# Eight attention steps placed among the groups of rows by a table, five buffers for the last tanh, and the last sums made in place

## The chip, the core and the metric

The kernel runs on one core of one Trainium2 chip, as one launch. The metric is the device time of an execution in microseconds. Before the change it is 1671.74 us, the median of three runs (1670.36 to 1673.09). The core has five engines that run their own instruction streams and meet only at semaphores: TensorE (PE, matrix products, written to the eight banks of PSUM), VectorE (DVE), ScalarE (ACT), GpSimd (POOL) and SyncE (SP, which here only issues DMAs, in program order, each after the waits that stand before it).

## The reference

Two layers work on `x` of 8 batches x 512 tokens x 256. The change touches only the second layer's attention, its mixture of experts, and the final product of the two:

```python
def _L1_attn_ref(x, ln_scale, ln_bias, wq, wk, wv):          # 16 heads of 16
    xn = _layernorm(x, ln_scale, ln_bias)
    q, k, v = heads(xn @ wq), heads(xn @ wk), heads(xn @ wv)
    probs = jax.nn.softmax(einsum('bhid,bhjd->bhij', q, k) / sqrt(256), axis=-1)
    return einsum('bhij,bhjd->bhid', probs, v) + xn
def _L1_ffn_ref(x, Wr, rb, W1, W2, W3, Ws1, Ws2, Ws3):       # 8 experts, the best 2 of each token, 1 shared
    w_full = softmax weights of the best 2 experts, 0 for the others
    h = (x @ W1) * silu(x @ W3)                              # per expert, 256 -> 512
    out = sum over experts of w_full * (h @ W2)              # 512 -> 256
    return out + ((x @ Ws1) * silu(x @ Ws3)) @ Ws2
x = x + s * g        # x before the layer, s: attention, g: silu of the ffn's output
```

## The kernel before

The change lies in one function, `layer1_attend_and_feed`, the kernel's last stage (from 733 us to the end of the profiled execution). It interleaves two kinds of work on all engines, so that one fills the other's waits.

**Attention.** A *quarter* g (0 to 31) is four heads of one batch. It has 8 *steps* u (0 to 7). In a step PE multiplies queries and keys into a bank pair (`scores`, L1500), and ACT takes the exponential of 128 x 1024 (`exps`, L1643) into one of two `prob` tiles. After every two steps PE multiplies the probabilities with the values (`weigh`, L1510; it stands in the steps 1, 4, 5 and 7). The maxima of the rows are found ahead of time: one `maxima` per step, numbered i = 0 to 255, in which PE multiplies into the bank pair M (`a_max_bank`, L1479) and DVE reduces it (L1786). There is one M, so PE may start maxima i only when DVE has reduced i - 1. In the step u = 3 PE transposes the maxima of the next quarter (`transpose_max`, L1486), DVE splits them in two rows (`split_max`, L1793 and L1795), and SP writes them into the query tile (`max_rows`, L1275 and L1278). In the steps 1 and 2 the outputs are copied (`copy_o`, ACT L1648), transposed (`transpose_o`, PE L1517) and divided (`divide`, DVE L1800 and L1804), and POOL adds them into `x_rows` (`add_o`, L1394). Query and key tiles (`qa`, `ka`) have three buffers: `load_qk(g + 2)` (six DMAs L1259 and six L1263, 64 KB each) is issued at the first step of quarter g, once the scores of quarter g - 1 are done, and is first needed by the maxima with i = 8 (g + 2).

**Groups of rows.** A *group* e (0 to 27) is 512 rows that go through an expert: 8 with the shared expert, 20 with rows sorted by expert. All its products are made as three products of split numbers (L93). In each of the group's places k = 0, 2, 4, 6 PE makes a quarter of gate and value (`up_gate`, `up_value`: 24 products, written to `a_hidden_bank`), and in k = 1, 3, 5, 7 a quarter of the down product of group e - 1 (`down`, 12 products). In k = 7 PE first transposes the next group's rows into M (`transpose_x`, L1525), ACT and DVE split them (`high_x` L1665, `low_x` L1822), and no maxima is made (in k = 4 there are two). Weights are loaded to `a_raw` by SP (L1285), split by ACT (`high_w`, L1672) and by POOL (`low_w`, L1408) or DVE (`low_w2`, L1827). A new weight's load waits until the old one is split; that of the second w2 of a group waits for the `low_w2` that DVE makes in place 6, after `low_h` (L1817). Each engine's order is written out by hand; there is one quarter per group, with g = e and u = k. SP's order in a group is: `load_qk`, the next rows, w3 and w1 of the next group, `load_v`, w2, `max_rows`, w3, w1 and w2.

**The end.** The last group is e = 27, so quarters 28 to 31, which is 32 steps, run after it. The down products of group 27 are made in quarter 28. Then ACT weights them (L1691), POOL adds them to the output array `fs` in memory by an indirect DMA (L1416), SP waits for these DMAs (`f_out`) and loads `fs` back in 8 batches (L1338; three semaphores, so batch 3 waits until batch 0 has landed), and for each batch b ACT takes tanh (`half_tanh`, L1679) and DVE does three operations (`last`, L1831, L1834 and L1839): (tanh + 1) x fs, times 0.5 x `x_rows`, plus `x1`. The tanh has two buffers, so that of batch b waits for the sum of batch b - 2. The sums go to three buffers, and SP stores each (L1347). DVE makes `last(0)` to `last(4)` after place 6 of quarter 30, `last(5)` and `last(6)` after that of quarter 31, and `last(7)` after `divide(31)`. From quarter 28 on the scores use two bank pairs, since the gate's banks are free.

## Time and profile before

| | us |
|---|---|
| median of three runs | 1671.74 |
| the profiled execution | 1671.11 |
| its span, first to last instruction | 1669.4 |
| PE busy in the span | 1505.7 (90%) |
| DVE, ACT, POOL busy | 1160.4, 963.8, 814.9 |
| mean granted TensorE clock | 0.956 of full |

A busy share is an average over stages. What is to be read here are two stretches: from 1090 to 1577 us, where groups of rows and attention run together, and from 1577.4 us (the first scores of quarter 28) to the end at 1669.4 us, where attention and the last sums run.

### The profile page before, as it was taken

The page shows a single profiled execution, that of the slowest core. Times are in us where ns is not written, and L with a number is a line of the kernel's source. Part 1 is how long each engine was busy: PE and PEld are TensorE (multiplying, and loading weights), DVE is VectorE, ACT ScalarE, POOL GpSimd, SP SyncE. Part 2 cuts the span into 40 slices and gives each one's busy share as a digit, 9 for nine tenths or more (in the row PEclk, how much of TensorE's full clock was granted, in tenths as well). Part 3 has the DMA queues.
Part 4 walks back from the last instruction along what each step waited for, and adds up shares of the span by engine and source line. Part 5 has one row for each costly group of instructions (what it writes and reads, how often), then busy time and mean ns, then how long its engine had stood idle before and what let it go on. Part 6 is the DMA issues. An engine that isn't in the chain of part 4 may idle for free.

```text
span 1669.4 us, 27215 instructions
## 1 busy us (share of the span) xinstructions
PE 1505.7 (90%) x9542; PEld 1128.7 (68%) x9542; DVE 1160.4 (70%) x1802; ACT 963.8 (58%) x1526; POOL 814.9 (49%) x755
## 2 busy tenths in 40 slices
PE   6589999999998379779999999999999999999976
PEld 3267877877787368647777777777777777777631
DVE  6667657757766388578776667777777777777657
ACT  3464565566454255434454567767677676777644
POOL 6424564554543278510255534656556655565410
PEclk9899999999999689969999999999999999999985
DMA  6716556553433579641455546766657677576563
GB/s 229 235 56 159 132 107 173 114 149 92 114 102 51 136 259 325 242 114 51 125 148 153 162 135 170 188 164 167 179 157 194 154 176 188 150 191 155 120 208 138
DMA packets 185384, 261.20 MB, mean 156 GB/s; under 512 B 36128, under 2 KB 117024, under 8 KB 185248
## 3 DMA queue, kind: packets, MB, share of 16 engines
q1 hardware_dynamic: 157216, 219.53, 43.8%
q0 software_dynamic: 28032, 39.93, 13.0%
q8 instruction: 77, 1.26, 0.3%
q14 instruction: 59, 0.48, 0.1%
HBM read 174.30 MB, written 84.56 MB: 155 GB/s over the span
## 4 chain that ended last, share of the span: by engine, by line
PE 39%; DVE 6%; SPq 3%; DMA 3%; issue 2%; ACT 2%; another core or an unknown queue 0%; POOL 0%; DVEq 0%; ACTq 0%; POOLq 0%
PE a_hidden_bank L93 16%; PE a_bank L93 8%; PE a_bank L1510 5%; PE a_max_bank L1479 5%; PE a_score_bank L1500 3%; DVE a_neg_max L1786 2%; DMA a_ka<-qk 2%; SPq L1259 1%; PE a_max_bank L1525 1%; SPq L1263 1%; PE a_bank L1517 1%; DVE a_w21lo L1827 1%; DVE a_hT1lo L1817 1%; ACT a_xThi L1665 1%; DVE a_w20lo L1827 1%
## 5 line engine op out<-in xcount | busy, mean ns | idle before, releaser
L1643 ACT ACTIVATE a_prob<-a_score_bank 128x1024 f32<-128x1024 f32 x240 | 246.2, 1026 | 244.7 <-PE a_score_bank L1500 198.6
L1786 DVE TENSOR_REDUCE a_neg_max<-a_max_bank 128x2 f32<-128x1024 f32 x249 | 304.1, 1221 | 82.4 <-PE a_max_bank L1479 70.5
L1416 POOL DMA_INDIRECT fs<-a_y,a_token x80 | 128.7, 1609 | 182.5 <-ACT a_y L1691 159.2
L619 POOL DMA_INDIRECT f<-e_ye,c_slot_row x64 | 104.6, 1635 | 128.7 <-ACT e_ye L530 65.6
L1479 PE MATMUL a_max_bank<-a_ka,a_qa 48*128 48x512 f32 x498 | 127.1, 507 | 27.8 <-DVE a_neg_max L1786 17.1
L1510 PE MATMUL a_bank<-a_prob,a_va 128*32 128x512 f32 x1024 | 143.3, 633 | 0.8 <-ACT a_prob L1643 0.6
L1809 DVE SCALAR_TENSOR_TENSOR a_tg<-a_tg,a_hidden_bank 128x512 f32<-128x512 f32 x112 | 76.7, 685 | 75.6 <-ACT a_tg L1653 71.0
L708 DVE TENSOR_TENSOR e_h<-e_bank,e_sge 128x512 f32<-128x512 f32 x64 | 44.3, 692 | 113.0 <-ACT e_sge L517 112.1
L1500 PE MATMUL a_score_bank<-a_qa,a_ka 50*128 50x512 f32 x480 | 100.5, 415 | 4.7 <-ACT a_prob L1643 2.4
L1479 PEld LDWEIGHTS a_max_bank<-a_ka,a_qa 48*128 48x128 f32 x498 | 47.5, 187 | 74.0 <-DVE a_neg_max L1786 31.1
L364 PE MATMUL e_bank<-m_wqkv,x_rows 128*128 128x512 f32 (+1 forms) x256 | 89.4, 492 | 4.6 <-ACT e_qkv L467 2.9
L1653 ACT ACTIVATE a_tg<-a_hidden_bank 128x512 f32<-128x512 f32 x112 | 67.2, 600 | 44.4 <-PE a_hidden_bank L93 38.2
L517 ACT ACTIVATE e_sge<-e_bank 128x512 f32<-128x512 f32 x64 | 38.2, 597 | 93.1 <-PE e_bank L93 92.0
L93 PE MATMUL a_hidden_bank<-a_xThi,a_w31hi 128*128 128x256 f32 x288 | 90.1, 313 | 0.0
L93 PE MATMUL e_bank<-e_w3hi,e_heThi 128*128 128x256 f32 x256 | 77.5, 303 | 13.6 <-DVE e_heTlo L712 13.6
L1813 DVE TENSOR_TENSOR a_h<-a_hidden_bank,a_tg 128x512 f32<-128x512 f32 x112 | 77.5, 692 | 15.3 <-PE a_hidden_bank L93 4.1
L93 PE MATMUL a_hidden_bank<-a_xThi,a_w11hi 128*128 128x256 f32 x288 | 85.0, 295 | 0.0
L611 POOL DMA_INDIRECT e_xg<-xn,c_slot_row x64 | 73.0, 1140 | 20.5 <-issue 19.2
L93 PE MATMUL a_hidden_bank<-a_xThi,a_w31lo 128*128 128x256 f32 x288 | 82.9, 288 | 0.0
L93 PE MATMUL a_hidden_bank<-a_xTlo,a_w31hi 128*128 128x256 f32 x288 | 82.7, 287 | 0.0
L93 PE MATMUL a_hidden_bank<-a_xTlo,a_w11hi 128*128 128x256 f32 x288 | 82.0, 285 | 0.0
L93 PE MATMUL a_hidden_bank<-a_xThi,a_w11lo 128*128 128x256 f32 x288 | 81.7, 284 | 0.0
(370 smaller groups left out, 4909.1 us busy)
## 6 DMA issues: line engine op xcount, KB each, us to landing
a_raw<-in_W SPq DMA_DIRECT2D x120, 512.0 KB
e_raw<-in_w SPq DMA_DIRECT2D x48, 512.0 KB, 4.1
a_qa<-qk SPq DMA_DIRECT2D x192, 64.0 KB
a_ka<-qk SPq DMA_DIRECT2D x192, 64.0 KB
xs<-c_pad SPq DMA_DIRECT2D x20, 516.0 KB
a_xg<-xs SPq DMA_DIRECT2D x20, 516.0 KB
qk<-p_hi SPq DMA_DIRECT2D x32, 256.0 KB, 4.0
qk<-p_lo SPq DMA_DIRECT2D x32, 256.0 KB, 4.3
```

What stands on the lines that cost most here:

```text
L93: ins = nc.tensor.matmul(out, a[i][x], b[l][y], start=first and n == m == 0, stop=last and n == len(pairs) - 1 and m == 2)
L364: ins = nc.tensor.matmul(bank[:, 0:f1 - f0], m.xnT[:, n, ch, t * P:(t + 1) * P], m.wqkv[:, ch, f0:f1], start=ch == 0, stop=ch == DC - 1)
L611: nc.gpsimd.indirect_dma_start(xg[u][:, t, :], None, xn_rows, bass.IndirectOffsetOnAxis(k.slot_row[:, e, t:t + 1], 0)).then_inc(xg_in[u], 16)
L619: nc.gpsimd.indirect_dma_start(f_rows, bass.IndirectOffsetOnAxis(k.slot_row[:, e, t:t + 1], 0), ye[:, t, :], None, compute_op=ALU.add).the ...
L1416: nc.gpsimd.indirect_dma_start(f_rows, bass.IndirectOffsetOnAxis(token[x % 4][:, t:t + 1], 0), y[:, t, :], None, compute_op=ALU.add).then_ ...
L1479: nc.tensor.matmul(max_bank(g, m)[:, s, :], qa[q][rows, p, t * P:(t + 1) * P], ka[q][rows, p, :], start=True, stop=True).then_inc(p1_ps, 1)
L1500: nc.tensor.matmul(score_bank(g, u)[:, s, :], ka[q][rows, p, j * P:(j + 1) * P], qa[q][rows, p, :], start=True, stop=True).then_inc(s_ps, 1)
L1510: ins = nc.tensor.matmul(OB[rows, :], va[g % NR][:, j, rows], prob[j % 2][:, h_, :], start=j == 0, stop=j == T - 1, tile_position=(0, 32 * ...
L1643: nc.scalar.activation(prob[j % 2][:, 2 * p:2 * p + 2, :], score_bank(g, u)[:], ACT.Exp, scale=float(D) ** -0.5).then_inc(p_done, 1)
L1786: nc.vector.tensor_reduce(neg_max[:, g % 2, :, T * p + t], max_bank(g, m)[:], AX.X, ALU.max, negate=True).then_inc(mx_done, 1)
L1809: nc.vector.scalar_tensor_tensor(tg[:], tg[:], 1.0, GATE[:], ALU.add, ALU.mult).then_inc(act_done, 1)
L1813: nc.vector.tensor_tensor(h[:], VALUE[:], tg[:], ALU.mult).then_inc(h_done, 1)
```

## The change

**A table of steps.** `steps` lists, for each of the 256 attention steps n = 8 g + u, the group and place (e, k) beside which it runs. The odd groups from 13 to 27 get a ninth entry with k = None: a step of attention with no group work, after place 7. So attention runs ahead of the groups by one step more after each, and 24 instead of 32 steps are left after group 27 (`freed` = 232). Up to group 13 the step u of a place k is the same as before; after that u = k + 1 (groups 14 and 15), k + 2 (16 and 17), and so on to k + 7 (26 and 27). `made[n]` is how many maxima have been made ahead of step n: 13 + n, and one more in the places 5, 6 and 7 and for the second maxima of place 4. Every engine's loop now runs over the table; work of the attention is tied to u, work of the groups to k. On SP `load_qk`, `load_v` and `max_rows` come at u = 0, 1 and 3, ahead of the group's loads of the same step.

**The end.** All eight loads of `fs` are issued at once, with one semaphore each for batch 0 and batch 1, one for 2 and 3, one for the rest. The tanh has five buffers (the three `raw` tiles, `xg` and `y`), and the product and the sum are written to `k.rows[:, b]`, from which they are stored. The tanh of batch 0 to 3 stands after the steps 247 to 250, that of 4 to 7 after 252 to 255; `last(0)` to `last(4)` stand in DVE's order at the steps 247, 249, 251, 253 and 255, the others behind them, with `divide(31)` ahead of `last(7)`.

```diff
-    th, sums = [raw[i][:].rearrange("p a f -> p (a f)") for i in range(2)], [raw[2][:].rearrange("p a (h d) -> p (a h) d", d=D), xg[:, :, 0:D], y[:]]
-    AHEAD = 3
+    th = [*(raw[i][:].rearrange("p a f -> p (a f)").rearrange("p (t d) -> p t d", d=D) for i in range(3)), xg[:, :, 0:D], y[:]]
+    TH = len(th)
...
+    rests = range(NF - 15, NF, 2)
+    steps = []
+    for e in range(G):
+        steps += [(e, k_) for k_ in range(NU)] + [(e, None)] * (e in rests)
+    steps = steps[:NU * G]
+    made = [LEAD]
+    for e, k_ in steps:
+        made.append(min(made[-1] + {4: 2, 7: 0}.get(k_, 1), NU * G))
+    freed = steps.index((NF, 0))
+    turned = [0] + [made[steps.index((e - 1, NU - 1))] for e in range(1, NF)]
...
@@ SP @@
-            for g in range(G):
-                e = g
-                if g + 2 < G:
+            for n, (e, k_) in enumerate(steps):
+                g, u = divmod(n, NU)
+                if u == 0 and g + 2 < G:
                     load_qk(g + 2)
-                store(e - 2, 1)
-                if group(e + 1):
-                    load_x(e + 1)
-                if NB <= e + 1 < NF:
+                if u == 1 and g + 2 < G:
+                    load_v(g + 2)
+                if u == 3 and g + 1 < G:
+                    max_rows(g + 1)
+                if k_ == 0:
+                    store(e - 2, 1)
+                    if group(e + 1):
+                        load_x(e + 1)
...
+                if k_ == 2 and NB <= e + 1 < NF:
                     load_w(0, weights(e + 1, 0))
                     load_w(1, weights(e + 1, 0))
...
+                if k_ == 3 and NB <= e < NF:
                     load_w(2, weights(e, 0))
...
                     for b in range(NB):
-                        sp.wait_ge(fs_in[b % AHEAD], 16 * (b // AHEAD))
-                        sp.dma_start(tiles(fs[b]), at(fs_b, b)).then_inc(fs_in[b % AHEAD], 16)
+                        sp.dma_start(tiles(fs[b]), at(fs_b, b)).then_inc(fs_in[batch_set(b)], 16)
...
@@ PE @@
+            for n, (e, k_) in enumerate(steps):
+                g, u = divmod(n, NU)
...
+                if k_ == 7 and group(e + 1):
                     transpose_x(e + 1)
+                if made[n + 1] > made[n]:
+                    maxima(made[n])
+                scores(g, u)
+                if u == 1 and g:
+                    weigh(g - 1, 3)
+                if u == 2 and g:
+                    transpose_o(g - 1)
+                if u == 3:
+                    transpose_max(g + 1)
+                if u in (4, 5):
+                    weigh(g, u - 4)
+                if u == 7:
+                    weigh(g, 2)
+                if k_ in (0, 2, 6) and group(e):
+                    up_gate(e, k_ // 2)
+                    up_value(e, k_ // 2)
...
+                if k_ in (1, 3, 5, 7) and group(e - 1):
+                    down(e - 1, k_ // 2)
...
@@ ACT @@
-                if b >= 2:
-                    act.wait_ge(sum_done, b - 1)
-                nc.scalar.activation(th[b % 2], fs[b], ACT.Tanh, scale=0.5).then_inc(th_done, 1)
+                if b >= TH:
+                    act.wait_ge(fin_done, 2 * (b - TH) + 2)
+                nc.scalar.activation(th[b % TH], tiles(fs[b]), ACT.Tanh, scale=0.5).then_inc(th_done, 1)
...
@@ DVE @@
-                nc.vector.scalar_tensor_tensor(th[b % 2], th[b % 2], 0.5, flat(k.rows[:, b]), ALU.mult, ALU.mult).then_inc(fin_done, 1)
+                nc.vector.scalar_tensor_tensor(k.rows[:, b], th[b % TH], 0.5, k.rows[:, b], ALU.mult, ALU.mult).then_inc(fin_done, 1)
                 dve.wait_ge(fin_done, 2 * b + 2)
                 dve.wait_ge(x1_in, 16 * NB)
-                if b >= 3:
-                    dve.wait_ge(out_done[b % 3], 16 * (b // 3))
-                nc.vector.tensor_tensor(sums[b % 3], tiles(th[b % 2]), tiles(x1[b]), ALU.add).then_inc(sum_done, 1)
+                nc.vector.tensor_tensor(k.rows[:, b], k.rows[:, b], tiles(x1[b]), ALU.add).then_inc(sum_done, 1)
```

Three places show what the table moves. On PE, between the last down product of place 7 of group 17 and the first gate product of group 18 (`a_max_bank` is a maxima, `a_score_bank` scores), there stood before:

```order
L93 MATMUL a_bank<-a_w21hi,a_hT0lo 128x256
L1479 MATMUL a_max_bank<-a_ka,a_qa 128x512 x2
L1500 MATMUL a_score_bank<-a_qa,a_ka 128x512 x2
L93 MATMUL a_hidden_bank<-a_xThi,a_w30hi 128x256
L93 MATMUL a_hidden_bank<-a_xTlo,a_w30hi 128x256
```

and now stand

```order
L93 MATMUL a_bank<-a_w21hi,a_hT0lo 128x256
L1497 MATMUL a_max_bank<-a_ka,a_qa 128x512 x2
L1519 MATMUL a_score_bank<-a_qa,a_ka 128x512 x2
L1536 MATMUL a_bank<-c_ident,a_oT 128x128 x4
L1497 MATMUL a_max_bank<-a_ka,a_qa 128x512 x2
L1519 MATMUL a_score_bank<-a_qa,a_ka 128x512 x2
L1504 MATMUL a_bank<-c_ident,a_neg_max 16x128
L93 MATMUL a_hidden_bank<-a_xThi,a_w30hi 128x256
L93 MATMUL a_hidden_bank<-a_xTlo,a_w30hi 128x256
```

Two maxima now stand close behind each other, with scores and a transpose between them and no product of a group. On DVE, at the same place (`a_xTlo` are the next rows, `a_w20lo` the w2 that place 6 splits), before:

```order
L1822 TENSOR_TENSOR a_xTlo<-a_max_bank,a_xThi 128x512 x2
L1817 TENSOR_TENSOR a_hT1lo<-a_h,a_hT1hi 128x2x256
L1827 TENSOR_TENSOR a_w20lo<-a_raw,a_w20hi 128x1024
L1786 TENSOR_REDUCE a_neg_max<-a_max_bank 128x2
L1809 SCALAR_TENSOR_TENSOR a_tg<-a_tg,a_hidden_bank 128x512
```

and now

```order
L1791 TENSOR_TENSOR a_xTlo<-a_max_bank,a_xThi 128x512 x2
L1786 TENSOR_TENSOR a_hT1lo<-a_h,a_hT1hi 128x2x256
L1796 TENSOR_TENSOR a_w20lo<-a_raw,a_w20hi 128x1024
L1755 TENSOR_REDUCE a_neg_max<-a_max_bank 128x2 x2
L1769 RECIPROCAL a_den<-a_bank 128x16
L1773 TENSOR_TENSOR a_o<-a_bank,a_den 128x256
L1778 SCALAR_TENSOR_TENSOR a_tg<-a_tg,a_hidden_bank 128x512
```

The first of the two reductions still stands behind the split of w2, and the second follows it at once. On SP, in group 22 (`a_raw` are weights, the one of 128x4x256 is w2; `a_vr` values, `a_mh` and `a_ml` the rows of maxima), before:

```order
L1285 DMA a_raw<-in_W 128x2x512
L1270 DMA a_vr<-v 128x4x64
L1283 TENSOR_LOAD c_owner
L1283 ISA x2
L1285 ISA
L1285 DMA a_raw<-in_W 128x4x256
L1275 DMA a_qa<-a_mh 1x8x128 x2
```

and now

```order
L1300 DMA a_raw<-in_W 128x2x512
L1274 DMA a_qa<-qk 16x2x512 x6
L1278 DMA a_ka<-qk 16x2x512 x6
L1298 TENSOR_LOAD c_owner
L1298 ISA x2
L1300 ISA
L1300 DMA a_raw<-in_W 128x4x256
L1285 DMA a_vr<-v 128x4x64
L1290 DMA a_qa<-a_mh 1x8x128 x2
```

The queries and keys of a quarter, which stood at the group's beginning, now come behind w3 and w1 and ahead of w2; in other groups they stand elsewhere in SP's order, by where u = 0 falls.

## Rows read from the trace of the kernel before

**Rows 1.** Windows: busy us of each engine (instructions), granted clock, DMA share, GB/s.

```profile
1577.40:1669.40 92.00, 60.75 (x309) 22.98 (x305) 58.72 (x61) 45.39 (x52) 15.64 (x13) 0.74 0.55 172
```

**Rows 2.** Timeline of PE, group 26 to 27: start, us, line, tiles [idle before].

```profile
1545.20 0.50 PE L1500 MATMUL a_score_bank<-a_qa,a_ka 50*128 50x512 f32 x2
1545.63 1.06 PE L1510 MATMUL a_bank<-a_prob,a_va 128*32 128x512 f32 x8
1548.26 0.50 PE L1479 MATMUL a_max_bank<-a_ka,a_qa 48*128 48x512 f32 x2
1548.60 0.39 PE L1500 MATMUL a_score_bank<-a_qa,a_ka 50*128 50x512 f32 x2
```

**Rows 3.** Timeline of DVE at the same place.

```profile
1547.86 0.69 DVE L1817 TENSOR_TENSOR a_hT0lo<-a_h,a_hT0hi 128x512 fp32r<-128x512 f32 x1 [0.63 <-ACT a_hT0hi L1659]
1548.47 1.22 DVE L1827 TENSOR_TENSOR a_w20lo<-a_raw,a_w20hi 128x1024 fp32r<-128x1024 f32 x1
1549.60 1.22 DVE L1786 TENSOR_REDUCE a_neg_max<-a_max_bank 128x2 f32<-128x1024 f32 x1
```

**Rows 4.** Timeline of PE: the two transposes of a quarter, in group 27.

```profile
1555.92 0.66 PE L1517 MATMUL a_bank<-c_ident,a_oT 128*128 128x128 f32 x4
...
1560.03 0.28 PE L1486 MATMUL a_bank<-c_ident,a_neg_max 128*16 128x128 f32 x1
```

**Rows 5.** Timeline of SP: starts of issues in groups 26 and 14.

```profile
1520.60 2.83 SPq L1259 DMA_DIRECT2D a_qa<-qk  x6
...
1528.58 2.73 SPq L1285 DMA_DIRECT2D a_raw<-in_W  x2
...
1534.09 0.39 SPq L1285 DMA_DIRECT2D a_raw<-in_W  x1
...
1158.22 4.94 SPq L1259 DMA_DIRECT2D a_qa<-qk  x6
```

**Rows 6.** Timeline of PE: maxima of places 2, 3, 5 and 6 of group 26.

```profile
1525.57 0.50 PE L1479 MATMUL a_max_bank<-a_ka,a_qa 48*128 48x512 f32 x2
...
1529.69 0.50 PE L1479 MATMUL a_max_bank<-a_ka,a_qa 48*128 48x512 f32 x2
...
1537.31 0.50 PE L1479 MATMUL a_max_bank<-a_ka,a_qa 48*128 48x512 f32 x2
...
1540.59 0.50 PE L1479 MATMUL a_max_bank<-a_ka,a_qa 48*128 48x512 f32 x2
```

**Rows 7.** Timeline of PE: two maxima that waited for keys.

```profile
1168.68 0.51 PE L1479 MATMUL a_max_bank<-a_ka,a_qa 48*128 48x512 f32 x2 [1.29 <-DMA a_ka<-qk]
...
1587.39 0.73 PE L1479 MATMUL a_max_bank<-a_ka,a_qa 48*128 48x512 f32 x2 [3.61 <-DMA a_ka<-qk]
```

**Rows 8.** Waits from 1100 to 1577 us: who for whom, us, times, longest.

```profile
PE a_max_bank L1479 <- DMA a_ka<-qk: 3.9, 6, 1.3
```

**Rows 9.** Windows: the stretch around the wait at 1587 us.

```profile
1585.00:1592.00 7.00, 4.61 (x25) 3.46 (x29) 3.07 (x5) 1.96 (x4) 0.68 (x1) 0.76 0.31 72
```

**Rows 10.** Timeline of SP and ACT, the last stretch.

```profile
1578.62 2.82 SPq L1259 DMA_DIRECT2D a_qa<-qk  x6
...
1615.37 0.33 SPq L1338 DMA_DIRECT2D a_w11hi<-fs  x1
...
1622.61 1.06 ACT L1679 ACTIVATE a_raw<-a_w11hi 128x1024 f32<-128x1024 f32 x1 [4.68 <-DMA a_w11hi<-fs]
...
1625.12 0.32 SPq L1338 DMA_DIRECT2D a_xTlo<-fs  x1
```

**Rows 11.** Timeline of PE and DVE, the last stretch.

```profile
1594.87 0.50 PE L1479 MATMUL a_max_bank<-a_ka,a_qa 48*128 48x512 f32 x2 [1.35 <-DVE a_neg_max L1786]
...
1629.92 1.20 DVE L1831 SCALAR_TENSOR_TENSOR a_raw<-a_raw,a_w11hi 128x1024 f32<-128x1024 f32 x1
...
1633.56 1.22 DVE L1831 SCALAR_TENSOR_TENSOR a_raw<-a_raw,a_w11lo 128x1024 f32<-128x1024 f32 x1
...
1660.69 0.26 DVE L1800 RECIPROCAL a_den<-a_bank 128x16 f32<-128x16 f32 x1 [3.88 <-PE a_bank L1517]
```

More of the change, by code:

```diff
@@ new lines, in _ @@
+            final = {freed + i: b for b, i in enumerate((15, 16, 17, 18, 20, 21, 22, 23))}
+            for n, (e, k_) in enumerate(steps):
+                g, u = divmod(n, NU)
+                fresh, coming = NB <= e < NF, NB <= e + 1 < NF
+                if k_ == 7 and group(e + 1):
+                    high_x(e + 1)
+                exps(g, u)
+                if u == 1 and g:
+                    copy_o(g - 1)
+                if k_ == 0:
+                    if group(e - 2):
+                        weighted(e - 2, 1)
+                    if group(e):
+                        tanh(e, 0)
+                    if fresh:
+                        high_w(0, weights(e, 1))
+                if k_ == 1:
+                    if group(e):
+                        high_h(e, 0)
+                    if fresh:
+                        high_w(1, weights(e, 1))
+                if k_ == 2:
+                    if e == 0:
+                        high_w(2, 0)
+                    if NB <= e - 1 < NF:
+                        high_w(2, weights(e - 1, 1))
+                    if group(e):
+                        tanh(e, 1)
+                if k_ == 3:
+                    if group(e):
+                        high_h(e, 1)
+                    if group(e - 1):
+                        weighted(e - 1, 0)
+                if k_ == 4:
+                    if group(e):
+                        tanh(e, 2)
+                    if coming:
+                        high_w(0, weights(e + 1, 0))
+                if k_ == 5:
+                    if group(e):
+                        high_h(e, 2)
+                    if coming:
+                        high_w(1, weights(e + 1, 0))
+                if n == NU + 5:
@@ L1770, in _ @@
-                exps(g, 7)
-                if group(e):
+                if k_ == 6:
+                    if group(e):
+                        tanh(e, 3)
+                    if fresh:
+                        high_w(2, weights(e, 0))
+                if k_ == 7 and group(e):
                     high_h(e, 3)
-                if e == NF + 1:
-                    half_tanh(0)
+                if n in final:
+                    half_tanh(final[n])
             copy_o(G - 1)
@@ L1930, in _ @@
             for m in range(NU):
-                maxima(0, m)
+                maxima(m)
             split_max(0)
-            for m in range(5):
-                maxima(1, m)
-            for g in range(G):
-                e = g
-                maxima(g + 1, 5)
-                if group(e):
+            for m in range(NU, LEAD):
+                maxima(m)
+            ending = {freed + i: b for b, i in enumerate((15, 17, 19, 21, 23))}
+            for n, (e, k_) in enumerate(steps):
+                g, u = divmod(n, NU)
+                if made[n + 1] > made[n]:
+                    maxima(made[n])
+                if u == 2 and g:
+                    divide(g - 1)
+                if u == 3:
+                    split_max(g + 1)
+                if k_ == 0 and group(e):
@@ L1951, in _ @@
-                if g:
-                    divide(g - 1)
-                if e == 0:
+                if n == 2:
                     low_w2(0)
-                if g == 1:
+                if n == NU + 2:
                     route_logit(1)
-                if g == 2:
+                if n == 2 * NU + 2:
                     route_slot(0)
-                if group(e):
+                if k_ == 2 and group(e):
                     hidden(e, 1)
-                maxima(g + 2, 0)
-                split_max(g + 1)
```

317 lines of the change are left out of this document (106 added, 211 removed).

## The prediction

> **What bounds the kernel now.** I read the page's busy lines first, then the clock and the windows by stage, then, at the seams that the table touches, the timelines of PE, DVE and SP, and last the waits. In the stage of groups and attention PE has no slack: a group takes some 30 us and PE's waits in 477 us of it are a few for keys and a few tenths elsewhere; those for keys sum to 3.9 us [rows 8]. So what PE must do or wait for there is time. After group 27 it is different: in 92.0 us PE is busy for 60.8 and the granted clock is 0.74 [rows 1]. There a chain sets the pace: down products of group 27, the add to `fs`, its loads, the tanh, eight times `last` on DVE. The change takes eight steps from the second stage to the first. The question is what a step costs beside PE's full list, and whether the last stage is paid by the step at all.
>
> **What an added step costs: work.** A step is one maxima and one scores, 0.34 us from start to start and about as much again [rows 2], so 0.7. Eight times that is 5.6. The added steps have u = 0 to 7, once each, so four of them weigh (1.06, some 1.0 of which is PE's own pace [rows 2]), one has the 0.6 transpose and one the 0.3 [rows 4]: 4.9. Together 10.5 us, at the full clock.
>
> **The wait between two maxima.** Take the scores of place 7 as time zero (1545.20). In the next step PE makes its maxima at 3.06, one weigh included [rows 2], but DVE reduces it only from 1549.60 to 1550.82, since `low_h` and the split of w2 stand ahead of it [rows 3]: until 5.6. Today 3 us of gate and value products cover that. In the added step nothing does: the next maxima needs the one M, and in the order there is only a scores between them. Another maxima that stood like this waited 1.35 us [rows 11]. So the second maxima starts at 5.7. PE is through at 2.0 (3.06 less the weigh) plus 0.7, plus what place 7 and the added step have of weighs and transposes: a gap of 3.0 less that. By u of the added step: 0: 2.0; 1: 2.0; 2: 1.4 and 0.5 more because the copy of the outputs (ACT) stands ahead of `high_h`; 3: 2.1 and 0.7 more for a `divide` behind the split; 4: 1.7 and 0.5 for `split_max`; 5: 1.0 and 0.4 (the exponential waits for a weigh); 6: 2.0. Sum 14.3. The eighth, after group 27, has no next rows and takes the place of a wait that is there today: 0.2 more than its work. Bounds: 8 if DVE's chain moves forward wherever ACT has less to do, 18 if it slips by another half microsecond each.
>
> **Two more seams.** With the shift, u = 2 falls on place 7 of group 18, so `divide` runs behind the split of w2 and ends at about 5.2, while PE stands at `transpose_max`, which needs it, at 3.3: 1.9. With u = 3 on place 7 of group 20 `split_max` ends at 5.05, and the weigh of the next step stands ready at 3.0: 2.0. Together 3.9; bounds 0 (if POOL's and ACT's lists give way) and 6.
>
> **The keys.** This is the largest term that the order alone doesn't show. Today `load_qk` starts when SP gets past the load of the second w2: 1520.60 in group 26 [rows 5], and is needed in place 3, at 1529.69 [rows 6], 9.1 us later. When PE did wait, the keys had taken 10.5 us (1158.22 to 1168.68) and 8.8 (1578.62 to 1587.39) [rows 5, 7]. I take 9.1: today they come just in time. The shift moves the need, not always the issue.
> - u = 0 on place 7 (groups 14, 15): SP is still behind the same w2, so the issue stays, but the need is a place earlier, 1525.57 instead of 1529.69 [rows 6]: 4.1 each. In the step after group 13 itself the seam's wait leaves 0.9.
> - u = 0 on place 4 (20, 21): SP is held by the first w2 until 1534.09 [rows 5] and issues behind it at 1534.5. Through the places 5 to 7 maxima run one ahead, so the need is place 6, 1540.59 [rows 6]: 6.1 us, short by 3.0 each.
> - u = 0 on place 3 (22, 23): behind w3 and w1, issued from 1528.58 to 1531.3 [rows 5], need in place 5, 1537.31 [rows 6]: 6.0, short by 3.1 each.
> - On places 6, 5, 2, 1 the issue is held only by the scores of the step before and has over 10 us: nothing.
>
> Sum 0.9 + 8.2 + 6.0 + 6.2 = 21.3, less the 3.9 that PE waits for keys today [rows 8], which falls away or is part of it: 17.4. Bounds: 5 (keys in 7 us, where no weight is ahead of them) and 28 (10.5 us). The weights that such a load pushes back (w2 in groups 22 and 23, by 3.4 us) are wanted by ACT only in place 6, and come just in time.
>
> **The clock.** After the wait of 3.61 us the two maxima took 0.73 instead of 0.50 [rows 7], and the granted clock of the 7 us around it is 0.76 [rows 9], so part of it ran at 1.2 instead of 2.4 GHz. Up to the next full-speed work that lost about 1.2 us. Seven new waits are of 1 to 4 us; I count 1.2 for half of the five or so longest: 3.0 (bounds 0 and 8). The Trainium skill (TensorE: Matmul & The Clock Gate, "What's actually happening") says that the gate follows how busy the array has been and halves the clock when it was idle. By it alone a wait costs more than its own length, and the trace agrees for the one of 3.61; for the short ones of [rows 8] it shows no loss.
>
> Rows in all: 10.5 + 14.3 + 0.2 + 3.9 + 17.4 + 3.0 = 49.3 us more until the scores after group 27.
>
> **What the last stage gets back.** Its first 8 steps are as before. The load of the last keys now starts about 1 us before the stage's zero and not 1.2 after (1578.62 against 1577.4 [rows 10]), because a step stands between it and the w2 that held it: the wait of 3.61 shrinks by 2.1, and 0.3 goes at the next maxima. The chain over POOL's add is unchanged. The `x1` loads no longer stand behind a `load_qk`, so they are out of the way when `fs` is loaded. Today batch 0 takes from 1615.37 to 1622.61, while two later batches were 2.5 us apart for two (1622.61 to 1625.12), 1.26 each [rows 10]. Alone it should land in some 3.5: 3.7 less. So the tanh of batch 0 comes at 45.2 (1622.61 less 1577.4) - 2.4 - 3.7 = 39.1 after the stage's zero and `last(0)` 1.1 later, at 40.2. Today DVE starts it at 52.5 (1629.92 [rows 11]), for it stands behind `divide(29)`; that wait of about 6 us goes. From there DVE bounds: a `last` takes 3.64 (1629.92 to 1633.56 [rows 11]), seven are 25.6, `divide(30)` 0.7, and from `divide(31)` to the end of the span it takes 8.7 as today (1660.69 to 1669.4): 35.0 instead of 39.5, the wait of 3.88 [rows 11] being gone. The remaining steps, 8 exponentials and 7 tanh of about 1 us and four weighs at the low clock, need under 20 and hide behind these 25.6. The five buffers are what lets ACT run ahead; that the sums are written elsewhere costs DVE nothing. The stage: 40.2 + 35.0 = 75.2 instead of 92.0, 16.8 less (bounds 11 and 21).
>
> The Trainium skill (DMA: Bandwidth & Descriptors, "Queues, rings and completion order") says that an engine takes the descriptors of one ring in order. By it batch 0 lands first though eight are issued at once; if they shared instead, it would land after 8 x 1.26 = 10.1 us and the gain be 6.6 smaller. The trace has three batches in flight, and shows them landing one after another, so I keep the smaller number.
>
> **The sum.** +49.3 - 16.8 = +32.5 us. The profiled execution took 1671.1 us (span 1669.4 and 1.7 around it), 0.6 less than the median. That gives 1703.6; I say 1703.
>
> **The rivals.**
> - *The keys come in time.* For it: in six waits of the whole stage the longest is 1.3 us, so the transfer may often be well under 9.1, and without weights ahead it has the 16 engines for itself. Against: the six that did wait show 8.8 to 10.5. Then 17.4 and the clock's 3.0 fall away: +28.9 - 16.8 = +12, 1683.
> - *Faster.* The mechanism: in the seam the reduction starts early enough, or PE had hidden slack there, so that a step costs its 10.5 / 8 = 1.3 us, and keys are in time; and the last stage is paid by the step, 92.0 / 32 = 2.9 each, 23 in all: -12.5, 1659. It decides from the point where the waits between two maxima and for keys together stay under 6 us. For it: ACT, DVE and the low clock do make a step dear there. Against: the chain over `fs` and the eight `last` does not have those steps in it.
> - *Dearer still.* The keys take 10.5 us as in group 14 (7 x 1.3 = 9 more) and the clock falls after each long wait (5 more): 1717.
>
> **Chances.** Forecast 0.60, keys in time 0.17, dearer 0.16, faster 0.07. What a measurement can tell from no change is 0.2%, 3.3 us. Faster than that 0.07, within it 0.03 (the low end of the second case), slower 0.90. The forecast's own range is 1693 to 1712. The one for 8 in 10 takes in most of the cheap case and the dear one's start: 1682 to 1716.
>
> **What would show it.** PE waiting for `a_neg_max` at eight places after groups 13, 15, ..., 27, by 1 to 3 us; PE waiting for `a_ka` in the groups after 14 and 15 by about 4 and in 20 to 23 by about 3; the stage's zero at 1627 instead of 1577; from there 75 us to the end, `last(0)` at 40, DVE then without a gap over 1 us but one. It is wrong if the waits for keys sum to under 8 us, if the two maxima stand under 2.2 us apart, or if the last stage gives back more than 25.

## The result and the profile after

The changed kernel takes 1727.4 us, the median of four executions (1719.0 to 1729.4), the kernel before, measured beside it, 1671.1 us (four). The ratio is 1.033, 95% interval 1.029 to 1.037. Forecast were 1703 us and a range of 1682 to 1716: the direction is right, the size is not. Of all executions in this document one, the fourth of e5_keys_where_shifted, took 1918 us at a granted clock of 0.736, and it is left out of every comparison.

The profiled execution is the shortest of the four, 1719.0 us with a span of 1717.3; the span grew by 47.9 us against a forecast of 32.5. Three windows say where. The first row is of before, from the transposes of group 14's rows (place 7 of group 13) to the last stage's zero, and the others are of after: the same stretch, and from that zero, the first scores after group 27's last work and the step behind it, to the end. Columns: window, its length, busy us of PE, its weight loads, DVE, ACT and POOL (instructions), granted clock, DMA share, GB/s.

```profile
1152.18:1577.40 425.22, 419.88 (x3120) 311.27 (x3120) 315.54 (x396) 298.81 (x407) 240.37 (x165) 1.00 0.65 167
```

```profile
1149.68:1641.98 492.30, 448.53 (x3190) 328.20 (x3189) 323.09 (x408) 305.25 (x416) 237.96 (x167) 0.96 0.58 146
...
1641.98:1717.30 75.32, 42.62 (x240) 16.67 (x236) 47.09 (x48) 36.60 (x43) 14.50 (x11) 0.75 0.61 198
```

The last stage answers to [rows 1]: 75.3 us instead of 92.0, as forecast (75.2). The stretch of rows is 67.1 us longer; it began 2.5 us earlier in this execution, so the zero moved by 64.6, where 49.3 had been forecast. The row splits the 67.1 in two. PE stood idle for 43.8 us (492.30 less 448.53) instead of 5.3, which is 38.4 more. And it was busy for 28.7 us more, though the added work was put at 10.5. The granted clock fell from 1.00 to 0.96, and the other 18.2 us are the same work at the half clock: in the clock's own record PE works for 37.8 us of the stretch at 1.2 GHz, which loses half of that, 18.9.

The idle time, by what PE waited for in that stretch (columns: who for whom, us in all, times, longest); it answers to [rows 8], where keys took 3.9 us in six:

```profile
PE a_max_bank L1497 <- DMA a_ka<-qk: 20.5, 6, 4.7
PE a_max_bank L1497 <- DVE a_neg_max L1755: 11.1, 8, 1.9
PE a_bank L1529 <- DVE a_ml L1764: 4.7, 2, 2.3
PE a_bank L1504 <- DVE a_o L1773: 4.2, 2, 2.1
PE a_max_bank L1497 <- issue: 1.8, 1, 1.8
PE a_score_bank L1519 <- ACT a_prob L1636: 1.3, 2, 0.8
```

One by one, in the timeline of PE (start, us, line, tiles, idle time before and what ended it); they answer to [rows 7]:

```profile
1156.32 0.51 PE L1497 MATMUL a_max_bank<-a_ka,a_qa 48*128 48x512 f32 x2 [1.89 <-DVE a_neg_max L1755]
1200.64 0.80 PE L1497 MATMUL a_max_bank<-a_ka,a_qa 48*128 48x512 f32 x2 [4.70 <-DMA a_ka<-qk]
1228.51 0.50 PE L1497 MATMUL a_max_bank<-a_ka,a_qa 48*128 48x512 f32 x2 [1.76 <-DVE a_neg_max L1755]
1235.87 0.50 PE L1497 MATMUL a_max_bank<-a_ka,a_qa 48*128 48x512 f32 x2 [1.66 <-DMA a_ka<-qk]
1326.93 0.27 PE L1504 MATMUL a_bank<-c_ident,a_neg_max 128*16 128x128 f32 x1 [2.08 <-DVE a_o L1773]
1360.38 0.27 PE L1504 MATMUL a_bank<-c_ident,a_neg_max 128*16 128x128 f32 x1 [2.07 <-DVE a_o L1773]
1389.31 0.75 PE L1497 MATMUL a_max_bank<-a_ka,a_qa 48*128 48x512 f32 x2 [3.64 <-DMA a_ka<-qk]
1426.33 0.50 PE L1497 MATMUL a_max_bank<-a_ka,a_qa 48*128 48x512 f32 x2 [3.25 <-DMA a_ka<-qk]
1463.94 0.50 PE L1497 MATMUL a_max_bank<-a_ka,a_qa 48*128 48x512 f32 x2 [2.94 <-DMA a_ka<-qk]
1499.53 0.80 PE L1497 MATMUL a_max_bank<-a_ka,a_qa 48*128 48x512 f32 x2 [4.33 <-DMA a_ka<-qk]
```

The six waits for keys are in groups 15, 16, 20, 21, 22 and 23, where the forecast had put all but one small one. The wait at 1228.51, of 1.76 us, shows what the forecast missed. The last of these windows is behind it, the first three are behind the long one at 1200.64:

```profile
1201.00:1203.00 2.00, 2.00 (x10) 1.35 (x9) 1.41 (x2) 1.07 (x2) 0.05 (x1) 0.50 0.69 228
1203.00:1205.00 2.00, 2.00 (x12) 2.00 (x11) 0.28 (x1) 1.12 (x2) 1.34 (x4) 0.50 0.01 2
1205.00:1207.00 2.00, 2.00 (x19) 1.49 (x18) 1.27 (x2) 0.37 (x1) 0.00 (x0) 0.98 0.03 6
...
1230.00:1232.00 2.00, 2.00 (x11) 2.00 (x11) 0.99 (x3) 1.20 (x3) 0.00 (x0) 0.50 1.08 263
```

PE is busy for all of each 2 us but gets through 10 to 12 matmuls at 0.50, which is 1.2 GHz, and 19 at full clock. There are ten such stretches in the rows' part: five at waits for keys (2.94 to 4.70 us), five behind waits in the seams (1.76 to 2.33 us). They cost some 1.8 us each (18.2 / 10).

The last stage, in the timelines of ACT, DVE and SP, answers to [rows 10, 11]:

```profile
1677.30 0.33 SPq L1355 DMA_DIRECT2D a_w11hi<-fs  x1
...
1681.48 1.06 ACT L1672 ACTIVATE a_raw<-a_w11hi 128x1024 f32<-128x1024 f32 x1 [5.48 <-DMA a_w11hi<-fs]
...
1682.57 1.23 DVE L1800 SCALAR_TENSOR_TENSOR a_raw<-a_raw,a_w11hi 128x1024 f32<-128x1024 f32 x1 [11.78 <-ACT a_raw L1672]
...
1711.71 1.23 DVE L1803 SCALAR_TENSOR_TENSOR x_rows<-a_raw,x_rows 128x1024 f32<-128x1024 f32 x1 [0.68 <-POOL x_rows L1409]
```

The load of batch 0 lands 4.2 us after its issue instead of 7.2, `last(0)` starts at 40.6 after the zero and 34.7 us remain. Behind it DVE has one gap, of 0.68 us.

### The profile page after: what moved, and what is told of

The parts are those of the page before. It is cut to its first block, busy times and chain, and to the rows that moved or that the text cites. A ratio compares the mean times of both kernels' runs of the same rounds, so it can differ in the third digit from the quotient of the medians.

```text
span 1717.3 us, 27212 instructions
## 1 busy us (share of the span) xinstructions
PE 1517.0 (88%) x9542; PEld 1140.8 (66%) x9542; DVE 1157.3 (67%) x1802; ACT 961.3 (56%) x1526; POOL 809.5 (47%) x755
## 4 chain that ended last, share of the span: by engine, by line
PE 39%; DVE 6%; DMA 3%; SPq 3%; issue 3%; ACT 2%; POOL 0%; ACTq 0%; DVEq 0%; POOLq 0%
PE a_hidden_bank L93 17%; PE a_bank L93 7%; PE a_bank L1529 5%; PE a_max_bank L1497 5%; PE a_score_bank L1519 3%; DMA a_ka<-qk 2%; PE a_max_bank L1545 1%; SPq L1274 1%; DVE a_neg_max L1755 1%; SPq L1278 1%; DVE a_w20lo L1796 1%; PE a_bank L1536 1%; ACT a_prob L1636 1%; DVE x_rows L1803 1%; ACT a_xThi L1658 1%
## 5 line engine op out<-in xcount | busy, mean ns | idle before, releaser
L1636 ACT ACTIVATE a_prob<-a_score_bank 128x1024 f32<-128x1024 f32 x244 | 250.1, 1025 | 266.6 <-PE a_score_bank L1519 210.7
L1782 DVE TENSOR_TENSOR a_h<-a_hidden_bank,a_tg 128x512 f32<-128x512 f32 x112 | 77.5, 692 | 14.3 <-PE a_hidden_bank L93 2.8
L1409 POOL TENSOR_TENSOR x_rows<-x_rows,a_o 128x256 f32<-128x256 f32 x32 | 29.8, 932 | 119.9 <-DVE a_o L1773 119.8
L611 POOL DMA_INDIRECT e_xg<-xn,c_slot_row x64 | 73.1, 1142 | 20.4 <-issue 19.2
```

The costliest lines, as they stand in the source:

```text
L611: nc.gpsimd.indirect_dma_start(xg[u][:, t, :], None, xn_rows, bass.IndirectOffsetOnAxis(k.slot_row[:, e, t:t + 1], 0)).then_inc(xg_in[u], 16)
L1636: nc.scalar.activation(prob[j % 2][:, 2 * p:2 * p + 2, :], score_bank(NU * g + u)[:], ACT.Exp, scale=float(D) ** -0.5).then_inc(p_done, 1)
L1782: nc.vector.tensor_tensor(h[:], VALUE[:], tg[:], ALU.mult).then_inc(h_done, 1)
```

## The experiments

Three questions were open: whether the six waits for keys and the seams cost what they seem to, what eight steps really return at the end, and whether a wait alone makes the clock fall. Theory at the start: rows and end are separate sums, and each wait costs its length and something for the clock. The main rival: the added steps cost so much for a reason that no single wait shows. Ratios are to the kernel before in the same batch of runs, with 95% intervals. Diffs are against the changed kernel unless another is named.

**e1_end_only: no added steps, the new end.**

```diff
-    rests = range(NF - 15, NF, 2)
+    rests = ()
...
-            final = {freed + i: b for b, i in enumerate((15, 16, 17, 18, 20, 21, 22, 23))}
+            final = {freed + i: b for b, i in enumerate((15, 16, 17, 18, 20, 24, 26, 28))}
...
-            ending = {freed + i: b for b, i in enumerate((15, 17, 19, 21, 23))}
+            ending = {freed + i: b for b, i in enumerate((19, 21, 23, 25, 27))}
```

> The changed kernel with an empty list of rests, so no added step: the groups run as before and 32 steps are left behind group 27. Kept: eight loads of fs at once, five tanh buffers, sums in the rows' tile. The tanh of the batches stand after the steps 15 to 18, 20, 24, 26 and 28 of the last stage and last(0) to last(4) at its steps 19, 21, 23, 25 and 27. Theory (the last stage is set by the chain of fs, tanh and eight last, not by its steps): last(0) starts at 48 to 50 us of the stage instead of 52.5 and runs without the wait of 3.9, so about 8 us faster than before, 1663 (1658 to 1667). Rival (what the last stage gave back was eight steps fewer): no gain, 1671 within 3. Second rival: the chip's time of the last stage falls by the full 15 us without the table, 1656.

Measured: 1670.2 us against 1673.8, ratio 0.997 (0.995 to 0.999). A gain between the rival's none and the theory's 8 us. Its last stage and the first `last`:

```profile
1588.65:1675.60 86.95, 55.31 (x309) 21.59 (x305) 58.53 (x61) 44.84 (x52) 15.65 (x13) 0.81 0.56 182
```

```profile
1640.97 1.20 DVE L1800 SCALAR_TENSOR_TENSOR a_raw<-a_raw,a_w11hi 128x1024 f32<-128x1024 f32 x1
```

The stage is 5.1 us shorter than before (92.0). The tanh of batch 0 (1634.12) comes 7.0 us after the issue of its load (1627.08); that this is due to the `x1` loads ahead of it is an inference here, which e8 tests. And `last(0)` starts at 52.3, still behind `divide(29)` and `split_max`. What the eight added steps return beside this end is then the difference to after: 86.95 less 75.32, 11.6 us, 1.45 a step. Their work is 10.5. So even at no wait at all they would have been worth 1 us, and less beside a better end (e8).

**e2_keys_first: all key loads ahead of the weights.** On SP, in every group:

```diff
-                if k_ == 2 and NB <= e + 1 < NF:
+                if k_ == 3 and NB <= e + 1 < NF:
                     load_w(0, weights(e + 1, 0))
...
-                if k_ == 3 and NB <= e < NF:
+                if k_ == 4 and NB <= e < NF:
                     load_w(2, weights(e, 0))
...
-                if k_ == 6 and NB <= e < NF:
+                if k_ == 7 and NB <= e < NF:
                     load_w(2, weights(e, 1))
```

> The changed kernel, but SP issues w3 and w1 of the next group in place 3, and the two w2 in places 4 and 7, instead of 2, 3 and 6, so that no weight that is held back stands ahead of a quarter's keys. Theory (waits for keys, and each long wait also loses about 1.7 us because the clock falls): the 20.5 us of waits for keys fall to under 4 and with them four or five stretches at the low clock: 25 us faster than the changed kernel, about 1702. Rival (a wait costs its length alone): 17 us faster, 1710. Rival (the weights are then late instead): not over 5 us faster.

Measured: 1745.1 us, ratio 1.044 (1.039 to 1.049). A miss, with the wrong sign: 18 us slower than the changed kernel where 25 faster was expected. The waits for keys fell from 20.5 to 2.4 us, but the groups 7 to 13, where the table had changed nothing, became 40.3 us longer (249.65 against 209.32). Window and waits of ACT and PE there:

```profile
942.42:1192.07 249.65, 223.28 (x1550) 167.52 (x1549) 150.85 (x193) 143.34 (x198) 109.45 (x81) 0.93 0.52 139
```

```profile
ACT a_w30hi L1665 <- DMA a_raw<-in_W: 46.6, 7, 7.2
```

```profile
PE a_score_bank L1519 <- ACT a_prob L1636: 24.1, 7, 4.1
```

With u = k, `max_rows` at u = 3 now stood ahead of the weights, and SP waits there for DVE's split of the maxima (`a_mh`): 31.6 us in these seven groups. ACT then stood at the split of w3 with the exponential behind it, and PE behind that. This stretch is also a measurement of the clock that nobody had planned: the same 1550 matmuls, seven waits of 2.8 to 4.1 us (and one of 1.5 for keys), and PE is busy for 223.3 instead of 208.2 us. Where the table does move steps (1192.07 to 1663.61), e2 did what it was made for: 471.5 us instead of 492.3.

**e3_maxima_moved: the added step makes no maxima.** Place 6 of those groups makes two instead, the second between its gate and value products, with the reduction at that place in DVE's order.

```diff
-        made.append(min(made[-1] + {4: 2, 7: 0}.get(k_, 1), NU * G))
+        made.append(min(made[-1] + {4: 2, 6: 1 + (e in rests), 7: 0, None: 0}.get(k_, 1), NU * G))
```

> The changed kernel, but the added step makes no maxima; place 6 of the same group makes two, one between gate and value products. So no two maxima stand close together after place 7. Theory (the one bank pair M and DVE's list make the second maxima wait): seven waits of about 1.8 us go, 10 to 12 us in all, and some low clock with them: 13 us faster than the changed kernel, about 1714. Rival (the scores then wait for the exponential of the added step instead, which DVE's wait had covered): 4 us faster, 1723.

Measured: 1733.0 us, ratio 1.034 (1.030 to 1.038): no gain, so theory and rival both miss. PE's waits from 1090 to 1640 us:

```profile
PE a_max_bank L1497 <- DMA a_ka<-qk: 29.7, 10, 6.6
...
PE a_max_bank L1497 <- DVE a_neg_max L1755: 2.2, 3, 1.0
```

The seam closed (2.2 us of waits for `a_neg_max` instead of 10.1 in the same window), and the keys, wanted one maxima earlier, took it back: 29.7 us instead of 20.5.

**e4_both: the edits of e2 and e3 together.**

> The two edits of e2_keys_first and e3_maxima_moved together. Theory: the gains add, and since fewer waits are left for the clock to fall in, a little more: 38 us faster than the changed kernel, about 1689, so still slower than before, by the work of eight steps (10.5 us), the waits for divide and split_max (9 to 10 us) and what clock is lost in them, less the 16 us of the last stage. Rival (waits cost their length alone): 28 us faster, 1699. Rival (they cover each other, so that with one gone the other grows): no more than the better of the two alone.

Measured: 1748.3 us, ratio 1.043 (1.037 to 1.048). A miss by 59 us: it inherits the late weights of e2, and its groups 7 to 13 take 257.1 us. In the stretch where the table moves steps (1203.09 to 1673.87) it takes 470.8 us, and e2 alone 471.5, against 492.3 in after. So the gains do not add there: the last rival's "no more than the better of the two alone" holds, with 6.9 us of waits for keys come back where e2 had 0.9.

**e5_keys_where_shifted: the reorder of e2 only where u = 0 falls behind a weight.**

```diff
-                if k_ == 2 and NB <= e + 1 < NF:
+                if k_ == (3 if e in (22, 23) else 2) and NB <= e + 1 < NF:
...
-                if k_ == 3 and NB <= e < NF:
+                if k_ == (4 if e in (20, 21) else 3) and NB <= e < NF:
...
-                if k_ == 6 and NB <= e < NF:
+                if k_ == (7 if e in (14, 15) else 6) and NB <= e < NF:
```

> The edit of e2_keys_first, but only in the groups where a held-back weight stands ahead of the keys: the second w2 in place 7 of groups 14 and 15, the first w2 in place 4 of groups 20 and 21, w3 and w1 in place 3 of groups 22 and 23. All other groups keep the changed kernel's order. Theory (keys and the clock): the waits for keys fall from 20.5 to under 4 us and the groups 15, 16 and 20 to 23 get 25 us shorter, as they did in e2_keys_first, with nothing lost elsewhere: 1702. Rival (a wait costs its length alone): 1710. Rival (SP's order costs elsewhere whatever one does): over 1715.

Measured: 1706.7 us, the median of three executions, ratio 1.017 (1.013 to 1.021), the profiled one 1708.3. From 1.033 that is 1.6%, 27 us, which would be the theory's 25; but the two ratios come from different batches, each with 0.4% either way. The stretch of rows and PE's waits (1090 to 1640 us):

```profile
1156.92:1632.87 475.95, 445.41 (x3189) 326.14 (x3189) 322.32 (x408) 304.92 (x416) 237.13 (x167) 0.97 0.60 151
```

```profile
PE a_score_bank L1519 <- ACT a_prob L1636: 5.9, 4, 2.7
...
PE a_max_bank L1497 <- DMA a_ka<-qk: 3.4, 3, 1.7
```

Between the two profiled executions the stretch gives 16.3 us: 13.2 of idle and 3.1 of the clock. The waits for keys gave 17.1, and 4.6 came back as waits for the exponential. The groups 15, 16 and 20 to 23 together are 19.2 us shorter (207.2 for 226.4), nearer to the rival's 17 than to the 24.0 that they gave in e2. So the keys' own part is shown, and the clock's part is not decided by this run.

**e6_split_behind: e5 (the diff is against it), and DVE splits w2 one place later in groups 18 to 21.**

```diff
-                if k_ == 6 and NB <= e < NF:
+                if k_ == (7 if e in range(18, 22) else 6) and NB <= e < NF:
                     low_w2(weights(e, 0))
```

> e5_keys_where_shifted, and DVE splits the first w2 of groups 18 to 21 in place 7, behind divide and split_max, instead of in place 6 ahead of them. Theory: the four waits of PE for a_o and a_ml, 8.8 us, fall under 1 us and four low-clock stretches of some 1.7 us lost each are less likely: 12 us faster than e5. Rival (waits cost their length alone): 8 us. Rival (the wait moves to the next maxima, which DVE then reduces later): under 3 us.

Measured: 1698.5 us, ratio 1.013 (1.010 to 1.016), 8 us less than e5 by the medians of the same batch, 6 by the ratios and 9 by the two profiled executions (1708.3 and 1699.0): nearer to the first rival's 8 than to the theory's 12. The waits for `a_ml` and `a_o` halved, 8.9 to 4.3 us, and 2.1 of that came back at the next maxima, as the second rival had it (waits for `a_neg_max` in the stretch: 13.2 us instead of 11.1):

```profile
PE a_bank L1529 <- DVE a_ml L1764: 2.4, 2, 1.2
PE a_bank L1504 <- DVE a_o L1773: 1.9, 2, 0.9
```

```profile
1150.92:1619.60 468.68, 442.51 (x3190) 324.08 (x3189) 322.64 (x408) 305.13 (x416) 239.04 (x167) 0.97 0.60 153
```

With the keys in time and this seam eased, the stretch is still 43.5 us longer than before: 20.8 idle and 22.6 busy, of which 12.1 are the clock.

**e7_before_late_keys: the kernel before, with one wait put in.** In ten groups SP issues the keys only after the scores of step 1.

```diff
                 if g + 2 < G:
+                    if 14 <= g < 24:
+                        sp.wait_ge(s_ps, 2 * (NU * g + 2))
                     load_qk(g + 2)
```

> The kernel before; only in groups 14 to 23 SP issues a quarter's queries and keys after the scores of step 1 of the group (it waits for their semaphore), some 2.4 us later than it does today, so that PE waits some 2.5 us for keys once in each of ten groups, and nothing else changes. Theory (a wait of about 2 us or more is followed by a stretch at the low clock): it costs the ten waits, 20 to 25 us, and 1.7 us more for each of at least half of them: 32 to 40 us slower than before, 1707. Rival (the clock only falls after long waits, such as 3.5 us): 20 to 25 us slower, 1694.

Measured: 1691.5 us, ratio 1.010 (1.007 to 1.013), half of what was expected, because the waits came out at 0.88 to 2.00 us. Stretch of rows, and two of the waits:

```profile
1151.81:1594.98 443.17, 426.21 (x3121) 315.29 (x3120) 315.70 (x396) 299.24 (x407) 241.08 (x165) 0.98 0.61 160
```

```profile
1200.13 0.80 PE L1481 MATMUL a_max_bank<-a_ka,a_qa 48*128 48x512 f32 x2 [2.00 <-DMA a_ka<-qk]
...
1296.12 0.50 PE L1481 MATMUL a_max_bank<-a_ka,a_qa 48*128 48x512 f32 x2 [1.24 <-DMA a_ka<-qk]
```

Here the work is exactly that of before, and PE is busy for 6.3 us more (426.2 against 419.9). It is nearly all in four groups, with waits of 2.00, 1.65, 2.00 and 1.55 us, 1.4 to 1.6 in each. The groups with waits of 0.88 to 1.27 us, and one with 1.76, are busy as before.

**e9_before_longer_waits: the same, after the scores of step 2.**

```diff
                 if g + 2 < G:
+                    if 14 <= g < 24:
+                        sp.wait_ge(s_ps, 2 * (NU * g + 3))
                     load_qk(g + 2)
```

> The kernel before, with one edit on SP: in groups 14 to 23 the keys of quarter g + 2 are issued only after the scores of step 2, so that PE has to wait for them in place 3 of these ten groups. It asks what a wait costs beside its own length. The earlier trial with the keys one step sooner left waits of 0.9 to 2.0 us, and those groups in which the clock stayed at full speed were longer by the wait alone, those in which part ran at 1.2 GHz by the wait and 1.2 to 1.6 us. Planned now: waits of some 4 to 5 us each, ten of them, 40 to 50 us. Theory (each wait of this length is followed by a stretch at 1.2 GHz that costs about 1.5 us, whatever the wait's length): the ten groups are longer by the sum of their waits plus 12 to 18 us, the group's PE busy time rises by 1.2 to 1.8, time about 1728. Rival (the clock's loss grows with the wait, about 0.4 us for each us waited): waits plus 20 us or more, 1735. Second rival (waits alone): PE busy time of the groups is unchanged, 1717.

Measured: 1724.0 us against 1670.8, ratio 1.032 (1.030 to 1.035). Ten waits of 3.9 to 4.1 us. The stretch, and in it two groups that follow each other:

```profile
1147.88:1629.38 481.50, 440.94 (x3120) 325.75 (x3120) 316.66 (x396) 298.79 (x407) 241.15 (x165) 0.95 0.57 147
```

```profile
1219.27:1255.68 36.41, 32.45 (x223) 23.68 (x222) 22.51 (x29) 21.34 (x30) 17.10 (x13) 0.91 0.54 142
1255.68:1290.78 35.10, 31.21 (x223) 23.43 (x222) 22.34 (x29) 21.34 (x30) 18.58 (x13) 0.95 0.56 147
```

Idle grew by 35.2 us and busy time by 21.1 for the same 3120 matmuls. That the wait costs more than itself is shown: the rival without any loss falls. Between the other two the run doesn't decide as planned. Their sums at the waits that came (12 to 18, and 0.4 x 39.5 = 16) are both below the 21.1 measured. In five of the ten groups PE was busy for 1.4 to 1.5 us more, in the five between them for 2.5 to 2.9 (32.45 against 29.74). So none of the ten was free, and the cheaper five cost what those half as long did in e7. The difference is how long the clock stayed low. Both windows begin 4.2 us behind the end of a wait, in group 16 and in group 17:

```profile
1242.60:1244.60 2.00, 2.00 (x12) 0.56 (x12) 1.93 (x2) 0.81 (x2) 0.33 (x1) 0.50 0.46 129
1279.00:1281.00 2.00, 2.00 (x18) 0.97 (x15) 1.23 (x1) 0.88 (x2) 1.59 (x3) 1.00 0.68 169
```

In the five dearer groups the clock fell while PE still waited, and it stayed low about twice as long as in the others.

**e8_end_x1_early: e1 (the diff is against it), with six of the `x1` loads at the stage's beginning and `last(0)` two steps earlier.**

```diff
+                if k_ == 1 and e == NF:
+                    sp.wait_ge(up_ps, FC * NF)
+                    for b in (0, 1, 2, 3, 6, 7):
+                        sp.dma_start(tiles(x1[b]), at(x1_b, b)).then_inc(x1_in, 16)
...
-            ending = {freed + i: b for b, i in enumerate((19, 21, 23, 25, 27))}
+            ending = {freed + i: b for b, i in enumerate((17, 19, 21, 23, 26))}
```

> e1_end_only, and SP loads six of the eight x1 batches at step 1 of the last stage, when the tiles of the gate and value weights are free, and the other two once the last down product is made; last(0) to last(4) stand at steps 17, 19, 21, 23 and 26. Theory (the first load of fs takes 7 us because the x1 loads stand ahead of it, and from last(0) on DVE bounds): fs lands 3 us sooner, last(0) starts at 44 instead of 52 us of the stage, and the end comes 5 to 7 us sooner than in e1_end_only: 1664, so faster than before by 0.4 to 0.6%. Rival (the attention steps then end last, since DVE holds up the maxima): 1669.

Measured: 1667.0 us against 1675.6, ratio 0.995 (0.993 to 0.997): faster than both kernels. Last stage and first `last`:

```profile
1583.19:1665.40 82.21, 51.83 (x309) 20.29 (x305) 58.33 (x61) 44.79 (x52) 15.66 (x13) 0.87 0.60 193
```

```profile
1626.95 1.22 DVE L1803 SCALAR_TENSOR_TENSOR a_raw<-a_raw,a_w11hi 128x1024 f32<-128x1024 f32 x1
```

`last(0)` starts at 43.8 after the zero, as expected, where e1 had 52.3, and the stage is 82.2 us, where e1 had 87.0 and before 92.0: 4.7 sooner than e1, a little under the 5 to 7 expected. Batch 0 of `fs` lands 3.3 us after its issue and not 7.0, which bears out that the `x1` loads had held it up. PE's 309 matmuls there took 51.8 us instead of before's 60.8, for the granted clock was 0.87 and not 0.74. So 9.8 of the 16.7 us that the change gets back at its end are to be had without moving a step, and the stage of after is only 6.9 us shorter than this one, less than the 10.5 that its steps cost elsewhere.

## Why the prediction was off

By its own steps, in the order of the sum.

- **Work, 10.5.** No run measured the sum by itself, and one group bears out its price. The stretch of group 24 (1508.43 to 1541.42 us of after), with an added step and its weigh, ran at full clock: PE was busy for 31.55 us against 29.75 before (1453.40 to 1483.61), 1.80 more, where 0.7 and 1.06 had been forecast. And the 28.7 us of added busy time less the 18.9 that the clock's record gives leave 9.8.
- **The wait between two maxima, 14.3.** Right. The seven seams show 1.89, 1.76, 1.84, 2.84 (2.07 and 0.77), 3.09 (2.33 and 0.76), 1.44 and 1.89: 14.8. Forecast by u were 2.0, 2.0, 1.9, 2.8, 2.2, 1.4 and 2.0.
- **Two more seams, 3.9.** Right: 2.08 at `transpose_max` in group 19, 2.34 at the weigh in group 21. e6 bears out the cause, DVE's split of w2, since both fell when it moved.
- **The keys, 21.3 less 3.9.** Near in size and right in place: 20.5 in six waits where seven had been forecast. Groups 20 to 23 show 3.64, 3.25, 2.94 and 4.33 for 3.0 to 3.1. Of the two at u = 0 on place 7, one is 4.70 and one 1.66 for 4.1 each, and the 0.9 after group 13 did not come. The time of 9.1 us was a little low: in before the six that waited had taken 9.4 to 10.5 us from issue to maxima (the 8.8 is from the last stage). e5 took 17.1 of them away, and the stretch got 16.3 us shorter.
- **Other waits.** 3.9 us, 1.4 of it in the seam after group 27, where 0.2 stood in the sum beside a wait that was there. Before had 1.4 of such small ones in this stretch.
- **The clock, 3.0, bounds 0 and 8.** This step failed. It took 18.2 us in the profiled execution, six times the forecast and over twice its upper bound. The text counted "1.2 for half of the five or so longest", from one example: the wait of 3.61 us [rows 7, 9] had a loss, and the short ones of [rows 8], up to 1.3 us, had none. Its "Seven new waits" fit its list for the keys alone. The nine waits in the seams, of 1.4 to 2.8 us, which it had forecast itself, passed as free, and seam waits brought five of the ten stretches; of the six waits for keys five brought one, not half. So in after ten stretches count at 1.8, in place of two and a half at 1.2: both factors were too small, the number by far the more. The trace of before had an example in between, in the same stage but ahead of the 1090 us from which the prediction read: a wait of 1.52 us in group 2, and the clock behind it.

```profile
807.51 0.50 PE L1479 MATMUL a_max_bank<-a_ka,a_qa 48*128 48x512 f32 x2 [1.52 <-DVE a_neg_max L1786]
```

```profile
809.50:811.50 2.00, 2.00 (x11) 2.00 (x11) 1.28 (x2) 0.91 (x1) 1.63 (x2) 0.50 0.09 10
```

PE was busy there for 31.34 us (788.33 to 821.28), and for 29.89 in e6, where the same wait had no such stretch behind it. Of the experiments, e7 puts such waits on the dear side: four of five of 1.55 to 2.00 us had a stretch at 1.2 GHz behind them, and cost 1.4 to 1.6 beside themselves. e9 gives 2.1 for each of ten waits of 4 us, e2 2.2 for each of seven (15.1 / 7). The rule that the prediction cited (the Trainium skill, TensorE: Matmul & The Clock Gate, "What's actually happening": idle time halves the clock) agrees in its direction; that by it any wait costs more than its own length does not hold here, since the waits of 1.66, 1.84, 1.89 and 2.34 us in after had no stretch at 1.2 GHz behind them.
- **The last stage, -16.8.** Right: -16.7, with `last(0)` at 40.6 for 40.2 and 34.7 for 35.0 behind it. Batch 0 landed 4.2 us after its issue with the others in flight, and they landed behind it in the order of their issue (5.0, 6.3 and 7.3 us after their own), so the reading of the queue (the Trainium skill, DMA: Bandwidth & Descriptors, "Queues, rings and completion order") agrees here: had the eight shared, it would have been 10.1. Inside it two parts were off and small: the wait for the last keys shrank to 2.20 us, where 1.5 had been forecast, and batch 0 took 4.2 for 3.5. How the 16.7 divide between the two halves of the change depends on the order of the end: 5.1 for the end and 11.6 for the steps by e1, 9.8 and 6.9 by e8.

The sum closes: 28.7 busy and 38.4 idle, less the 2.5 by which the stretch began earlier, less 16.7, is 47.9. The 15.4 us by which it misses 32.5 are 15.2 of the clock and 2.6 of waits, less the 2.5.

What is open: the median of after is 8.4 us above its profiled execution. The mean granted clocks of the four executions are 0.948, 0.945, 0.944 and 0.941, at 1719.0, 1725.8, 1729.4 and 1729.1 us, so it is likely that the others lost more to the clock, but only one has a trace. Also open is what decides whether a wait of some 2 us brings the low clock at all, and whether it stays low once or twice as long, as in e9.

The rival "faster" took a step to cost 1.3 and to return 2.9. It returns 1.45 (e1 against after) and 0.9 beside the end of e8, so with every wait gone, the move would be near zero or a small loss.

## What to carry to other kernels

Where TensorE is the bound and runs without a gap, price new waits of some 2 us and more at one and a half times their length together: their own time, and work behind them at half the clock. (38.4 us of added idle time came with 18.2 in after, 35.2 with 21.1 in e9, 11.6 with 6.3 in e7.) A single wait of 2 us can cost nothing beside itself or some 1.5 us. Ask of an example of a cost in the trace what lies between it and the cases shown to be free, look for such a case in the rest of the stage too, and put the bound where nothing has been measured yet. Before work is moved into such a stage, measure what the other stage returns with the rest of the change alone; and an issue order on a DMA queue is to be changed only in the iterations that have the problem, since it holds for the others as well.

## What the runs showed of the hardware

The eleven traces together, from 800 us to the last stage, each stretch at 1.2 GHz counted to the longest wait of PE close to its beginning: of 59 waits of 0.8 to under 1.5 us none had one, of 63 of 1.5 to 2.4 us 42 had one, and all 40 of 2.5 us or more had one. Between 1.5 and 2.4 us the same wait goes either way. That of group 2, 1.50 to 1.52 us in every kernel, brought the low clock in before, after and e9 and in none of the other eight. In after those of 1.66 (1235.87), 1.84 (1294.30), 1.89 (1577.87) and 2.34 us (1401.06) did not, while in e5 that of 1.84 (1294.00), that of 1.89 (1567.21) and that of 2.33 us (1396.96) did. In e9 all of the ten waits, equal within 0.3 us, had one, and the loss still came in two sizes, alternating from group to group, with the length of the stretch. A wait's length alone doesn't fix its price.
